# Eight instead of seven gathered blocks in a graph layer, and a row table added up by GpSimd on chip

## The reference

```python
def gnn(x, edge_index, W, b, prelu_a):          # called on layernorm(x)
    src, dst = edge_index, each with one more loop per node
    deg = segment_sum(ones_like(dst), dst)
    norm = rsqrt(deg)[src] * rsqrt(deg)[dst]
    h = x @ W
    out = segment_sum(h[src] * norm[:, None], dst) + b
    return where(out > 0, out, prelu_a * out)

x = x + gnn(layernorm(x), stack([src, dst]), W, b, prelu_a)
z = layernorm(x)
# ffn(z): softmax over 8 experts from the mean row, the best 2 of them,
# gelu(z @ W1 + b1) @ W2 + b2 weighted, plus z, then a layer norm with gamma and beta
x = x + ffn(z)
```

## Time and profile before

| | us |
|---|---|
| median of 3 runs | 1013.46 |
| lowest and highest | 1009.28 and 1021.48 |
| the profiled execution | 1019.87 |
| its span, first to last instruction | 1017.9 |

### The profile page before, as it was taken

One profiled execution on the slowest core, in us unless ns is written; L12 is line 12 of the kernel. 1 busy time (PEld: TensorE's weight loads), 2 busy tenths in 40 slices (PEclk: granted clock), 3 DMA queues, 4 the chain that ended last, 5 costly groups with the idle time before them and its releaser, 6 DMA issues.

```text
span 1017.9 us, 20363 instructions
## 1 busy us (share of the span) xinstructions
PE 991.0 (97%) x6991; PEld 839.4 (82%) x6992; DVE 844.9 (83%) x1720; ACT 514.9 (51%) x1006; POOL 532.6 (52%) x505
## 2 busy tenths in 40 slices
PE   8989989999999999999999999999899999999997
PEld 7767768888888888888888888888799999999996
DVE  6788868789988989989989889885777887878786
ACT  6486434444444444444444444443865647474641
POOL 4061288888888888888888888812001111111111
PEclk9799999999999999999999999999899999999999
DMA  9039956666666667657766666636211111111101
GB/s 306 14 106 270 180 135 153 160 159 155 159 155 157 167 146 170 160 124 171 163 148 163 160 155 159 149 68 234 74 33 53 41 46 46 46 46 46 45 22 36
DMA packets 70593, 126.76 MB, mean 125 GB/s; under 512 B 9876, under 2 KB 49934, under 8 KB 70510
## 3 DMA queue, kind: packets, MB, share of 16 engines
q0 software_dynamic: 33520, 90.35, 38.5%
q1 hardware_dynamic: 36990, 35.32, 10.9%
HBM read 66.93 MB, written 25.67 MB: 91 GB/s over the span
## 4 chain that ended last, share of the span: by engine, by line
PE 90%; DVE 4%; ACT 2%; issue 2%; DMA 1%; DVEq 0%; ACTq 0%; SPq 0%; POOLq 0%; another core or an unknown queue 0%
PE banks L1988 47%; PE banks L2097 13%; PE banks L1964 12%; PE banks L2111 8%; PE banks L2116 4%; PE banks L1829 3%; PE banks L1935 1%; DVE hot_src L1008 1%; PE banks L1819 1%; ACT gf L1759 0%; ACT gh L1757 0%; DVE hot_key L1008 0%; DMA dst_all<-in_dst 0%; ACT tab L1628 0%; DMA raw<-in_pairs,starts 0%
## 5 line engine op out<-in xcount | busy, mean ns | idle before, releaser
L1988 PE MATMUL banks<-tab,adj 128*128 128x512 f32 x2058 | 513.5, 399 | 1.3 <-ACT adj L1711 1.3
L1988 PEld LDWEIGHTS banks<-tab,adj 128*128 128x128 f32 x2058 | 375.1, 189 | 74.4 <-DVE tab L1121 1.5
L1706 ACT CAST adj<-banks 128x784 fp32r<-128x784 f32 x328 | 253.9, 815 | 334.6 <-PE banks L1964 314.9
L816 POOL DMA_INDIRECT fetched<-h_rows,node_row x252 | 318.4, 1263 | 76.5 <-issue 73.4
L1008 DVE TENSOR_TENSOR hot_src<-iota_src,turned 128x2048 bf16<-128x2048 bf16 x168 | 205.1, 1221 | 56.0 <-PE banks L1964 52.9
L1964 PEld LDWEIGHTS banks<-hot_key,hot_src 128*128 128x128 bf16 x2624 | 126.6, 98 | 47.2 <-issue 35.8
L1008 DVE TENSOR_TENSOR hot_key<-iota_key,turned 128x1568 bf16<-128x1568 bf16 x168 | 162.7, 969 | 0.0
L1964 PE MATMUL banks<-hot_key,hot_src 128*128 128x98 bf16 x2624 | 151.4, 209 | 4.5 <-issue 3.1
L2111 PE MATMUL banks<-W2s,gh 128*128 128x512 f32 x384 | 137.5, 399 | 0.5 <-DVE pre L1524 0.5
L1757 ACT ACTIVATE gh<-banks,b1e 128x384 fp32r<-128x384 f32 (+1 forms) x136 | 78.3, 575 | 88.7 <-PE banks L2097 88.5
L2116 PE MATMUL banks<-W2s,gl 128*128 128x256 f32 x392 | 110.0, 280 | 0.0
(11 more groups left out here) (257 smaller groups left out, 1103.5 us busy)
## 6 DMA issues: line engine op xcount, KB each, us to landing
partial<-fetched POOLq DMA_DIRECT2D x63, 512.0 KB
xin<-in_x SPq DMA_DIRECT2D x49, 128.0 KB
x_dram<-x SPq DMA_DIRECT2D x49, 128.0 KB
x1f<-x_dram POOLq DMA_DIRECT2D x16, 384.0 KB, 3.7
out<-res SPq DMA_DIRECT2D x48, 128.0 KB, 1.7
h_rows<-tab SPq DMA_DIRECT2D x5, 1024.0 KB, 15.0
h_rows<-tab POOLq DMA_DIRECT2D x5, 1024.0 KB, 15.1
W1a<-in_W POOLq DMA_DIRECT2D x8, 512.0 KB, 6.2
```

Of the source, the lines that this page charges most:

```text
L816: g.indirect_dma_start(out=into, out_offset=None, in_=h_rows, in_offset=bass.IndirectOffsetOnAxis(ap=node_row[:, k, r - 1:r], axis=0), bou ...
L1706: s.copy(adj[k][:, :].rearrange("p (q n) -> p q n", n=P)[:, :, at:at + 2 * BANK_NODES].rearrange("p q (b n) -> p q b n", b=2), bank_pairs[ ...
L1988: last = mm(acc[k][:, :], adj[k][:, q * P:(q + 1) * P], tab[:, q, :], start=(at == 0), stop=(at == T - 1), skip_group_check=True)
```

## The change

GATHERED becomes eight blocks (10, 15, ..., 45), one in five instead of one in six, so 41 blocks are dense. A node's list holds 35 rows instead of 39, all by indirect DMA; the own row comes from `tab` by an addition on VectorE. Rows are fetched in seven groups of five (the first to `partial`) with two buffers instead of three, eight in a slot from slot 1 on. Up to 256 extra edges for a block are taken in two chunks: two loads of sources, two indirect DMAs of rows and two accumulating matmuls for each block, and twice the matmuls and one-hot operations that place them. The row table is now made by 17 additions on GpSimd (16 of three blocks and one of one block) in one of two buffers, and each is stored by SyncE; the six stores and six adding DMAs, the wait of SyncE for the table and the loads of own rows are gone. The tiles of x lie in their buffer turned by 24 places, and the two adjacency buffers change places, as the number of dense blocks is odd now. `node_row` keeps the lists of all blocks.

```diff
-SUMMED = 39
-GFIRST, GCYCLE = 9, 6
-FETCH_FROM = 2
-WIDE = 4
-GROUPS = (SUMMED + 1) // WIDE
-FETCHED = 3
-ROOM = 26 * 1024 + 256
+SUMMED = 35
+CHUNKS = 2
+GFIRST, GCYCLE = 10, 5
+FETCH_FROM, PACE = 1, 8
+WIDE = 5
+GROUPS = SUMMED // WIDE
+FETCHED = 2
+ROOM = 27 * 1024
...
-    TABLE_PARTS = ((0, 8), (HELD, 32), (8, 16), (32, 40), (16, HELD), (40, T))
+    TABLE_PARTS = [(at + 3 * j, at + 3 * j + 3) for j in range(HELD // 3) for at in (HELD, 0)] + [(T - 1, T)]
...
     def rounds(i):
-        m, j = divmod(i - FETCH_FROM, SLOTS_PER)
-        n = GROUPS * WIDE
-        return [(m, r) for r in range(max(1, n * j // SLOTS_PER), n * (j + 1) // SLOTS_PER)] if 0 <= m < NGATH else []
+        at = (i - FETCH_FROM) * PACE
+        return [divmod(j, SUMMED) for j in range(max(0, at), min(at + PACE, NGATH * SUMMED))]
+
+    def rows_listed_at(m):
+        return 2 * m - 2
...
+        def row_sums(i):
+
+            lo, hi = TABLE_PARTS[i]
+            return summed_rows[:, i % 2, 0:hi - lo, :]
+
+        def rows_stored(eng):
+
+            for k in range(2):
+                eng.wait_ge(row_sums_stored[k], len(TABLE_PARTS[k::2]) * 16)
...
-            def load_own(m):
-                d = GATHERED[m]
-                sp.dma_start(partial[:, m % 2, 0, :], h_rows[d * P:(d + 1) * P, :]).then_inc(own_in[m % 2], 16)
-
             with sp.If(is_dense(sp)):
                 for d in range(2):
                     sp.dma_start(xin[:, d, :], x[d * P:(d + 1) * P, :]).then_inc(tile_by_sp[d], 16)
                 for i, (lo, hi) in enumerate(TABLE_PARTS):
-                    if lo < HELD:
-                        sp.wait_ge(hi_fixed, hi)
-                    else:
-                        sp.wait_ge(hi_made, hi - HELD)
-                    sp.dma_start(h_rows[lo * P:hi * P, :].rearrange("(t p) d -> p t d", p=P), tab[:, lo:hi, 0:D].bitcast(F32)).then_inc(hi_stored[i // 2], 16)
-                sp.wait_ge(h_summed, 16 * len(TABLE_PARTS))
-                for m in range(2):
-                    load_own(m)
+                    sp.wait_ge(row_sums_made, i + 1)
+                    sp.dma_start(h_rows[lo * P:hi * P, :].rearrange("(t p) d -> p t d", p=P), row_sums(i)).then_inc(row_sums_stored[i % 2], 16)
                 for d in range(T):
                     sp.wait_ge(epi, d * EPI + (2 * EPI + 5))
                     sp.dma_start(x1_dram[d * P:(d + 1) * P, :], x1[:, d % 2, :]).then_inc(x1_by_sp[d % 2], 16)
                     if d + 2 < T:
                         sp.dma_start(xin[:, d % 2, :], x[(d + 2) * P:(d + 3) * P, :]).then_inc(tile_by_sp[d % 2], 16)
-                    if d in GATHERED[:NGATH - 2]:
-                        load_own(GATHERED.index(d) + 2)
...
                 def load_extra_rows(m):
...
                     k = m % 2
                     if m >= 2:
                         pool.wait_ge(extra_summed, m - 1)
-                    g.indirect_dma_start(
-                        out=extra_row[:, k, :], out_offset=None, in_=h_rows,
-                        in_offset=bass.IndirectOffsetOnAxis(ap=extra_src[:, m:m + 1], axis=0),
-                        bounds_check=last_row).then_inc(extra_row_in[k], 16)
-
-                def add_low_rows(i):
+                    for c in range(CHUNKS):
+                        g.indirect_dma_start(
+                            out=extra_row[:, k, c, :], out_offset=None, in_=h_rows,
+                            in_offset=bass.IndirectOffsetOnAxis(ap=extra_src[:, c, m:m + 1], axis=0),
+                            bounds_check=last_row).then_inc(extra_row_in[k], 16)
+
+                def make_row_sums(i):
                     lo, hi = TABLE_PARTS[i]
                     if lo < HELD:
                         pool.wait_ge(lo_fixed, hi)
                     else:
                         pool.wait_ge(lo_made, hi - HELD)
-                    pool.wait_ge(hi_stored[i // 2], 32)
-                    g.dma_start(h_rows[lo * P:hi * P, :].rearrange("(t p) d -> p t d", p=P), tab[:, lo:hi, D:2 * D].bitcast(F32),
-                                accum_op=ALU.add).then_inc(h_summed, 16)
+                    if i >= 2:
+                        pool.wait_ge(row_sums_stored[i % 2], i // 2 * 16)
+                    g.tensor_tensor(row_sums(i), tab[:, lo:hi, 0:D].bitcast(F32), tab[:, lo:hi, D:2 * D].bitcast(F32), ALU.add).then_inc(row_sums_made, 1)
                 def fetch_round(m, r):
                     k, group = m % 2, r // WIDE
-                    if r == 1:
+                    if r == 0:
                         pool.wait_ge(node_row_made, m + 1)
                         if m >= 2:
                             pool.wait_ge(epi, GATHERED[m - 2] * EPI + (2 * EPI + 2))
...
                             pool.wait_ge(group_added, (n - FETCHED + 1) * 16)
                     g.indirect_dma_start(
                         out=into, out_offset=None, in_=h_rows,
-                        in_offset=bass.IndirectOffsetOnAxis(ap=node_row[:, k, r - 1:r], axis=0),
+                        in_offset=bass.IndirectOffsetOnAxis(ap=node_row[:, m, r:r + 1], axis=0),
                         bounds_check=last_row).then_inc(landed, 16)
                 def add_group(m, group):
...
                     k, n = m % 2, group_number(m, group)
                     pool.wait_ge(fetched_in[n % FETCHED], (n // FETCHED + 1) * 16 * WIDE)
                     if group == 1:
-                        pool.wait_ge(own_in[k], m // 2 * 16 + 16)
-                        pool.wait_ge(partial_in[k], (m // 2 + 1) * 16 * (WIDE - 1))
+                        pool.wait_ge(partial_in[k], (m // 2 + 1) * 16 * WIDE)
                     if n:
                         pool.wait_ge(group_added, n * 16)
                     g.dma_start(partial[:, k, :, :], fetched[:, n % FETCHED, :, :], accum_op=ALU.add).then_inc(group_added, 16)
...
                     load_edges(q)
                 for m in range(2):
                     load_node_src(m)
-                pool.wait_ge(extra_edge_made, 1)
+                pool.wait_ge(extra_edge_made, CHUNKS)
                 for m in range(NGATH):
-                    load_extra_src(m)
+                    for c in range(CHUNKS):
+                        load_extra_src(m, c)
                 for i in range(len(TABLE_PARTS)):
-                    add_low_rows(i)
-                pool.wait_ge(h_summed, 16 * len(TABLE_PARTS))
-                pool.wait_ge(extra_src_in, 16 * NGATH)
+                    make_row_sums(i)
+                rows_stored(pool)
+                pool.wait_ge(extra_src_in, 16 * CHUNKS * NGATH)
                 for i in range(ND):
                     if i % 2 and i + 5 < ND:
                         load_edges((i + 5) // 2)
-                    if (i - FETCH_FROM) % SLOTS_PER == 3 and (i - FETCH_FROM) // SLOTS_PER + 1 in range(2, NGATH):
-                        load_node_src((i - FETCH_FROM) // SLOTS_PER + 1)
+                    for m in range(2, NGATH):
+                        if i == rows_listed_at(m):
+                            load_node_src(m)
                     for m, r in rounds(i):
                         fetch_round(m, r)
-                        if r % WIDE == WIDE - 1:
-                            if r // WIDE > 1:
-                                add_group(m, r // WIDE - 1)
-                            elif r // WIDE == 0 and m:
-                                add_group(m - 1, GROUPS - 1)
-                        if r == SUMMED:
+                        if r // WIDE > 1 and r % WIDE == 1:
+                            add_group(m, r // WIDE - 1)
+                        if r == 2 and m:
+                            add_group(m - 1, GROUPS - 1)
+                        if r == SUMMED - 1:
                             load_extra_rows(m)
                 add_group(NGATH - 1, GROUPS - 1)
...
-                            extra_end[:, :].rearrange("p (m o) -> p m o", o=1).to_broadcast([P, NGATH, P]), ALU.is_ge).then_inc(before_extra_made, 1)
+            v.tensor_scalar(wide_node[:, :], extra_end[:, :], float(CHUNKS * P), None, ALU.is_gt, ALU.add, accum_out=over_wide[:, :]).then_inc(lost_made, 1)
+            for c in range(CHUNKS):
+                v.scalar_tensor_tensor(out=before_extra[:, c, :, :], in0=iota[:, :].rearrange("p (o n) -> p o n", o=1).to_broadcast([P, NGATH, P]), scalar=float(c * P),
+                                       in1=extra_end[:, :].rearrange("p (m o) -> p m o", o=1).to_broadcast([P, NGATH, P]),
+                                       op0=ALU.add, op1=ALU.is_ge).then_inc(before_extra_made, 1)
...
                 def one_hot_extra(m):
-                    v.tensor_scalar(hot_extra[:, m % 2, :], iota[:, :], extra_node[:, m:m + 1], None, ALU.is_equal).then_inc(hot_extra_made, 1)
+                    for c in range(CHUNKS):
+                        v.tensor_scalar(hot_extra[:, c, :], iota[:, :], extra_node[:, c, m:m + 1], None, ALU.is_equal).then_inc(hot_extra_made, 1)
                 def add_partials(m):
                     k = m % 2
```

(23 more changed lines are left out.)

85 lines of the change are left out of this document (47 added, 38 removed).

## The result

| | kernel before | changed kernel |
|---|---|---|
| median (lowest to highest), us | 1013.61 (1009.28 to 1021.48) | 1042.88 (1036.87 to 1045.22) |
| the profiled execution, its span | 1019.87, 1017.9 | 1040.58, 1038.9 |

The ratio is 1.027, 95% interval 1.019 to 1.035: slower, clear of noise, though this interval does not settle whether by more than 2%. Beside other kernels, in the third set of experiments on another chip, the same kernel came out at 1.036 (1.032 to 1.040). The forecast of 1031 (1002 to 1048) has the sign, the mechanism and, between the two profiled executions, most of the size: +18.2 forecast, +20.7 measured. A second profiled execution of the changed kernel, further down, is 32.4 us longer in span than the one of before, so how close the two sizes lie owes something to the execution.

The account below looks back on a forecast made before the run. TensorE, busy 97% of the span, was taken to bound the kernel. Its path -9.7 us plus 27.9 us of GpSimd lateness gave +18.2: 1038 on the profiled run, 1031 on the median, range 1002 to 1048.

Parts of the forecast that it names:

- GpSimd without a pause, late at the end: Dense stage: GpSimd has no wait but issue from the first fetch; VectorE waits 27.9 us for late gathered sums; chance 0.45.
- the rival: Row table's additions on GpSimd starve VectorE: some 16 us late on TensorE's path, 1020 to 1026 us; chance 0.12.
- First fetch 134.8: After the row table: GpSimd's first row fetch at 134.8 us, 10.6 later than before, bounds 113.6 to 152.3.
- GpSimd's work 561.1: From the first fetch on: GpSimd's operations sum to 556.1 us, 13.2 more than before, plus 5 for larger additions and two buffers.
- the 3 that were put down: Group additions of 640 KB with two fetch buffers: their landing holds GpSimd's fetches 3 us in sum.
- Head room 11.1: End of the dense stage: GpSimd's last sum had 11.1 us to spare, 6.7 at VectorE and 4.4 before TensorE's count.
- VectorE's 6.7: Last gathered block, kernel before: VectorE takes the last addition 6.7 us after it has landed.
- its 4.4 us: Last gathered block, kernel before: TensorE counts with VectorE's next one-hot pair 4.4 us after that pair ends.
- TensorE's path -9.7: TensorE's own work: -14.6 us for one dense block fewer, +3.9 for extra edges, +1.0 for the prologue.
- the first rival: GpSimd is in time and TensorE's path decides: 1004 us, or 998 if the early stall does not recur; chance 0.20.
- From the profiled execution to the median: 1038 on the profiled run; the runs' median was 6.4 lower, so 1031.7, rounded to 1031.
- VectorE starved, "but it hides inside POOL's lateness": Row table's additions hold up VectorE, some 16 us; deciding only where GpSimd (POOL) is late by less; chance 0.12.

Follow-up runs that it names:

- third set of experiments: Four kernels run beside the kernel before (median 1013.3 us) on one chip, among them the changed kernel unaltered: 1050.95 us, ratio 1.036.
- taking 73 us of its work away: Changed kernel with 30 instead of 35 fetched rows a node, the last five left out, and seven instead of eight fetches a slot: 1019.3 us, ratio 1.001.
- taking 14: Changed kernel with the second chunk's extra-edge rows neither fetched nor multiplied in the dense stage: 1038.1 us, ratio 1.026.
- With both costs gone: Changed kernel with 30 rows a node, seven fetches a slot, and the row table made by stores and adding DMAs: 998.5 us, ratio 0.982.
- the two pairs where nothing else is late: Table on chip against by DMA: kernel before, 1031.3 us with it on chip (ratio 1.018); changed kernel with 30 rows, seven a slot, 1019.3 against 998.5.
- the run with the table by DMA: Changed kernel with the row table made the old way, by SyncE's stores and GpSimd's adding DMAs in DRAM: 1041.0 us, ratio 1.027.
- the first run with 512 KB: Changed kernel with each adding DMA over four of five rows, 512 instead of 640 KB, in the second set: 1033.9 us, ratio 1.016.
- 30 rows: Changed kernel with 30 rows a node and seven fetches a slot, table on chip against by DMA: 1019.3 and 998.5 us, ratios 1.001 and 0.982.
- seven blocks: Kernel before, with its seven gathered blocks, its row table made by GpSimd's 17 additions on chip: 1031.3 us, ratio 1.018.
- In pieces of 128x256: Changed kernel with each three-block table addition cut into three of one block, 49 in place of 17: 1053.5 us, ratio 1.034.

## Why the prediction was right

Point by point, by its own steps, against the first profile of the changed kernel:

- **GpSimd without a pause, late at the end.** Right: VectorE waits at the last three gathered blocks, taking 73 us of its work away gives some 25 us of time back (16.7 of them its lateness at the end, 6.3 an earlier start), and taking 14 gives 13. Two of its signs failed: the first fetch was to come after 130, and GpSimd was to have no wait but issue; and two signs of the rival showed beside it, the long one-hots and TensorE waiting for them.
- **First fetch 134.8.** It was 126.5, mis-sized by 8.3. The loads of sources ended at 79.2, not 82.9, since most issue in 1.01 us; and 16 spacings to 119.6 make 2.5 us, not 2.8, the 384 KB stores landing in 2.5. An addition by itself is 1.79 us (taken: 1.7). The estimate from the Trainium skill (GPSIMD Engine Reference, section 3.1) was 1.7 to 1.8; the trace agrees.
- **GpSimd's work 561.1.** From 126.54 to 695.87 it is 569.3, 8.2 more. 4.1 of them are the wait for the freed sum; without it a fetch is (454.4 - 4.1) / 280 = 1.608 instead of 1.572 us, 10.2 in all, and the other instructions together take 6 us less than forecast. Larger additions cost nothing in issue, 1.006 against 1.011 us, and their landing holds the fetches for 6.7 instead of 2.1 us, against the 3 that were put down. The errors of the first fetch and of the work cancel by chance: forecast end 695.9, measured 695.87.
- **Head room 11.1.** By the forecast's terms the last partial sum comes 10.6 + 13.2 + 5 - 6.7 = 22.1 us later than before; measured 22.5, so VectorE's 6.7 held. TensorE's part did not come back whole: the span grew by 21.0, so 1.5 of its 4.4 us are seen. This is the mis-sized term that makes +18.2 of +20.7. The trace says where the rest went: from the last partial sum to TensorE's next count it is 3.5 us (700.8 to 704.3) in place of 6.9, 3.4 us gained; but after the wait the granted clock is 0.66 between 705 and 710, and the 12 matmuls of the table sum from 705.06 on take 4.59 us, where those from 685.95 on took 3.00 before.
- **TensorE's path -9.7.** Half of what it was, without an effect on the forecast, since GpSimd decided. With both costs gone it was 21.7 between the profiled spans (996.2 against 1017.9) and 19.1 between the medians. The rest, between the profiled spans, is what the first rival named, the stall of the kernel before at 124 to 146 and a late beginning: from 99.8 to its fourth dense block the kernel before takes 45.5 us, the other from 93.9 on 40.1. That beginning is also one of an execution with a granted clock of 0.66 between 35 and 50 us beside one with 1.00.
- **From the profiled execution to the median.** Here the forecast of 1031 lost most: the 6.4 us by which the execution of before lay above its median were taken off the changed kernel too, whose profiled execution lay 2.3 below its own. A profiled execution can be on either side, and the changed kernel moves from 1036.9 to 1052.0 over two chips.
- **VectorE starved, "but it hides inside POOL's lateness".** The mechanism and its price were right (16 forecast, 18 at the start of the dense stage, 18 and 21 in the medians of the two pairs where nothing else is late). That it hides was only partly so. In the run with the table by DMA, with its first fetch later, taking the starving away bought nothing; but through the freed partial sum GpSimd loses 4 us in one profile and 17 in the other. The forecast said that GpSimd would wait for nothing but its own issue; the step left out was the wait at the head of `fetch_round`, whose other side is VectorE. The Trainium skill (SBUF — State Buffer, "Who interferes with whom") has the second engine blocked until the first one's instruction is finished; the one-hots longer by 1.6 and by 0.54 us agree.

What stays open: why one execution's dense stage begins 11 us behind another's. In the second profile of the changed kernel VectorE's work on the table (L1134, L1140) lies beside the additions until 114.9 us, in the first until 95.8, and TensorE's granted clock between 80 and 100 us is 0.66 against 0.83. But the two part earlier, before any addition. Between 35 and 50 us, first and second profile:

```profile
35.00:50.00 15.00, 14.98 (x116) 12.48 (x114) 13.33 (x74) 8.71 (x32) 2.29 (x2) 1.00 0.13 37
35.00:50.00 15.00, 13.96 (x83) 11.22 (x84) 8.87 (x44) 5.20 (x18) 0.00 (x0) 0.66 0.00 1
```

TensorE gets through 83 matmuls in place of 116, and GpSimd's first addition comes at 83.0 in place of 79.2. With eight gathered blocks and additions of three blocks the dense stage begins at 111.4 and 117.7 us at a clock of 1.00 there, at 122.3 to 129.1 below it, but for the first run with 512 KB (0.66 and 118.0); with the table by DMA it begins at 93.9 to 103.7 at 1.00 and at 110.6 below it. Pairs of like clock give the additions on chip the same price, 17.5 us (30 rows, 1.00), 18.5 (35 rows, 0.66) and 18.7 (seven blocks, 0.66). What makes the clock fall in some executions was not tried; the kernel before has it too.

## What to carry to other kernels

An engine that is late decides alone only while nothing it waits for can be late too: before a cost is put down as hidden behind a late engine, go through each wait of that engine and ask whether the hidden cost delays its other side. Work taken from a queue laid out by slots can cost time, if the slots move ahead of what frees their buffers; change the amount and the pace together. And a block moved from the bound engine to another is worth its price only if the other has the room at the end of the stage: here 14.6 us less on TensorE stood against 26 us more of GpSimd's time (569.3 against 542.9), wanted 10 us earlier, from an engine with 11 to spare. And before two profiled executions are laid side by side, see whether their granted clocks were alike ahead of the stage in question: here that alone went with 11 us of the dense stage's start.

## What the runs showed of the hardware

VectorE operations with one tensor input were held up by the additions as well, in the changed kernel's first profile: the decoding step L1220 (a tensor_scalar of 128x128) took 1.84 us against a mean of 0.22 between 500 and 740 us, and L1224, with two, 1.92. In pieces of 128x256 the same steps took 0.75 and 0.83. A DMA that adds 640 KB is issued by GpSimd in the same 1.01 us as one of 512 KB. Single indirect fetches took GpSimd up to 4.7 us, where 1.17 is the median.
